# A graph network's attention pass: who tells the DMA queue that a ring slot is free

## The chip, the cores and the metric

The kernel runs on one core of one Trainium2 chip, in one launch. The metric is the device time of that core in microseconds. Three executions of the kernel before took 8953.53, 8963.97 and 8964.85 us; the median is 8963.97 us.

## The reference, cut to what matters

Four graph networks follow each other on 4096 nodes with 256 features and 65536 edges, sorted by target node: five message layers, a weighted graph convolution, an attention layer with 8 heads, and three normalised convolutions, each block closed by `x = layernorm(x + block(x))`. The change touches the attention layer alone:

```
h = (x @ W).reshape(n, 8, 32)
alpha = leaky_relu(a_src[src] + a_dst[dst], 0.2)
ex = exp(alpha - segment_max(alpha, dst)[dst])
coef = ex / (segment_sum(ex, dst)[dst] + 1e-16)
out = segment_sum(h[src] * coef, dst) + bias
```

## The kernel before, in words

The edges are cut into tiles of 128, and 8 tiles make an octet (`U = 8`). There are 64 octets. `ring` holds four octets of gathered rows, one in each slot. Octets are walked by a hardware loop over 16 groups with four octets (`ob`) written out in each.

A sum over edges that share a target is a matrix product with a one-hot matrix: VectorE builds, for a block of 128 target nodes, the matrix "edge e goes to node n", and TensorE multiplies it with the rows. An octet whose targets lie in one block needs one such unit of 8 matmuls, an octet that straddles two blocks needs two. How many blocks an octet touches is data: each engine that needs it loads it from `span_row` into a register (`span_of`, L210 to L219) and branches on it.

The attention layer has two passes over the edges. The first gathers the rows, writes them to `rows_table` and finds each node's maximum. The second, `attend_pass` (L599), reads the rows back octet by octet. Its engines do this:

- SP loads an octet's rows into its slot (L642) as soon as `rows_used` says that the slot is free. TensorE set `rows_used` to 4 at the kernel's start, so the first four loads wait for nothing of this pass.
- VectorE, in step h: multiplies the 8 tiles of octet h by their exponents (L841), adds the sums that TensorE finished last to `AGG` (L786), builds the first one-hot matrices of octet h+2 (`look_up_first`, L629), works out the logits of octet h+1 (`exponents`, L818 to L826), builds the second unit's one-hots of octet h if it has one, adds again, and builds the second unit's one-hots of octet h+2 if it has one.
- ScalarE takes the exponential of octet h+1 (L758) and copies the turned one-hots of octet h+2 out of PSUM (L751).
- TensorE, in step h: six of the eight matmuls of octet h's first unit (`sums`, L712), the transposes of octet h+2's one-hots (`turn_first`, L658), the last two matmuls, a second unit of sums if octet h has one, and then `find_all(h+2)`: it fetches each edge's target values by a product with the turned one-hots. `find_all` loads the octet's span into registers (L679), waits until VectorE has read the bank `psO` for the octet before (`logits`, L683), opens the bank's accumulation with a matmul of zeros (L685), does the products (L670), with another round of transposes where there is a second unit (L690), and closes with a matmul of zeros that signals `octet_found` (L693).

Between the sums of step h and `find_all(h+2)` stands L734, which is the line of the change:

```
pe.drain().then_inc(rows_used, 1)
ahead(pe, i, ob, 2, find_all)
```

The drain holds TensorE's sequencer until all its matmuls are done, and then tells SP that octet h's slot is free. `ahead` leaves `find_all` out in the last two octets. The waits of `attend_pass` on TensorE are on semaphores that VectorE and ScalarE raise (`weighed`, `b_made`, `b_added`, `a_made`, `a_copied`, `logits`).

Of the kernel before, what the change touches and what calls it, by code (L numbers as in the profile page):

```python
# [11 lines left out]
P = 128  # L12
# [10 lines left out]
U = 8  # L23
# [17 lines left out]
def build(nc, x, src, dst, edge_attr, edge_weight, vn_emb0, We, be, W1, b1, W2, b2, bn_g, bn_b, bn_m, bn_v,  # L41
# [3 lines left out]
    with ctx:  # L45
# [3 lines left out]
        def pb(name, shape):  # L49
            return ctx.enter_context(nc.psum_tensor(name, shape, F32))  # L50

        def sem(name):
            return ctx.enter_context(nc.semaphore(name))
# [83 lines left out]
        psO = pb("psO", [P, 512])  # L137
# [22 lines left out]
        rows_used = sem("rows_used")  # L160
# [37 lines left out]
        def flat(ap):  # L198
            return ap.rearrange("p a b -> p (a b)")
# [17 lines left out]
        def span_of(eng, h):  # L217

            v = eng.value_load(span_row[0:1, bass.ds(2 * h, 1)], min_val=NB, max_val=NB * NB + NB - 1)  # L219
            lo = nc.s_assert_within(v & (NB - 1), 0, NB - 1,  # L220
                                    skip_runtime_bounds_check_because="the low bits")
            cnt = nc.s_assert_within(v >> (NB.bit_length() - 1), 1, NB,
                                     skip_runtime_bounds_check_because="1 to NB blocks")
            return eng.snap(lo), eng.snap(cnt)
# [374 lines left out]
        def attend_pass(loads):  # L599
            W = 3 * 2 * HEADS  # L600
            found = small[:, 0:U * 2 * HEADS].rearrange("p (u h) -> p u h", u=U)
            zeros = stk_f[:, 3 * U * P // 2:2 * U * P].bitcast(BF16)[:, 0:U * W]
            turnedS = [psE[:, 512 * g:512 * g + 256].bitcast(BF16) for g in range(2)]

            def high(ap):

                halves = ap.bitcast(BF16).rearrange("p (e two) -> p e two", two=2)
                return halves[:, :, 1:2].rearrange("p e o -> p (e o)")

            def sums_bank(eng, c):  # L610

                start = nc.s_assert_within((c & U) * (512 // U), 0, 512,
                                           skip_runtime_bounds_check_because="0 or 512")
                return psAT[:, bass.ds(eng.snap(start), AW)]

            def in_range(b):
                return nc.s_assert_within(b, 0, NB - 1, skip_runtime_bounds_check_because="a block of the octet")

            def ahead(eng, i, ob, by, work):

                if ob < OB - by:
                    work(i, ob + by)
                else:
                    with eng.If(i < NG - 1):
                        work(nc.s_assert_within(i + 1, 0, NG - 1, skip_runtime_bounds_check_because="i < NG - 1"),
                             ob + by - OB)
# [7 lines left out]
            with nc.Block() as block:  # L634
                @block.sync
                def _(sp):

                    with sp.Fori(0, NG) as i:
                        for ob in range(OB):

                            sp.wait_ge(rows_used, OB * i + ob + 1)
                            sp.dma_start(octet_rows(ob), rows_table[bass.ds((OB * i + ob) * P, P), :]  # L642
                                         ).then_inc(rows_in[ob], 16)
                    loads(sp)

                @block.tensor
                def _(pe):
                    pe.reg_mov(na_pe, 0)
                    pe.reg_mov(nb_pe, 0)
                    pe.reg_mov(nx_pe, 0)  # L650

                    def turn(ob, c):
                        for g in range(2):
                            pe.wait_ge(a_made, c + 4 * g + 4)

                            pe.wait_ge(a_copied, c + 4 * g + 4)
                            for u in range(4 * g, 4 * g + 4):
                                ins = nc.tensor.transpose(turnedS[g][:, P * (u % 4):P * (u % 4) + P],  # L658
                                                          high(S_of[ob][:, u, :]), ident_b[:, :])
                            ins.then_inc(a_turned, 4)  # L660

                    def turn_first(i, ob):

                        turn(ob, pe.snap(na_pe))

                    def find(b, c):
                        for g in range(2):
                            pe.wait_ge(a_copied, c + U + 4 * g + 4)
                            for u in range(4 * g, 4 * g + 4):
                                ins = nc.tensor.matmul(psO[:, W * u:W * (u + 1)], ST[:, P * u:P * u + P],  # L670
                                                       flat(tgt[:, :, :])[:, bass.ds(b * W, W)],
                                                       start=False, stop=False)
                            ins.then_inc(a_found, 4)
                        pe.reg_add(na_pe, na_pe, U)

                    def find_all(i, ob):

                        h = OB * i + ob
                        lo, cnt = span_of(pe, h)  # L679
                        pe.reg_mov(cnt_pe[ob], cnt)  # L680
                        if not (isinstance(h, int) and h == 0):

                            pe.wait_ge(logits, h)  # L683

                        nc.tensor.matmul(psO[:, 0:U * W], zeros[:, 0:P], zeros, start=True, stop=False)  # L685
                        find(lo, pe.snap(na_pe))
                        with pe.If(cnt > 1):
                            with pe.Fori(1, cnt) as j:
                                c = pe.snap(na_pe)
                                turn(ob, c)  # L690
                                find(in_range(lo + j), c)

                        nc.tensor.matmul(psO[:, 0:U * W], zeros[:, 0:P], zeros, start=False, stop=True  # L693
                                         ).then_inc(octet_found, 1)


                    pe.wait_ge(zeros_ready, 1)
                    for ob in range(2):
                        turn_first(0, ob)
                        find_all(0, ob)  # L700
                    with pe.Fori(0, NG) as i:
                        for ob in range(OB):
                            h = OB * i + ob

                            def sums(c, first, u0, u1):
                                bank = sums_bank(pe, c)
                                for u in range(u0, u1):
                                    if first:
                                        pe.wait_ge(weighed, U * h + u + 1)
                                    elif u % 4 == 0:  # L710
                                        pe.wait_ge(b_made, pe.snap(nx_pe) + u + 4)
                                    ins = nc.tensor.matmul(bank, S_of[ob if first else OB][:, u, :],  # L712
                                                           ring[:, U * ob + u, 0:AW],
                                                           start=(u == 0), stop=(u == U - 1))
                                    if u % 4 == 3:
                                        ins.then_inc(b_used, 4)

                            c = pe.snap(nb_pe)

                            pe.wait_ge(b_added, c + U)  # L720
                            sums(c, True, 0, U - 2)

                            ahead(pe, i, ob, 2, turn_first)
                            sums(c, True, U - 2, U)
                            pe.reg_add(nb_pe, nb_pe, U)
                            cnt = pe.snap(cnt_pe[ob])
                            with pe.If(cnt > 1):
                                with pe.Fori(1, cnt):
                                    c = pe.snap(nb_pe)
                                    pe.wait_ge(b_added, c + U)  # L730
                                    sums(c, False, 0, U)
                                    pe.reg_add(nx_pe, nx_pe, U)
                                    pe.reg_add(nb_pe, nb_pe, U)
                            pe.drain().then_inc(rows_used, 1)  # L734
                            ahead(pe, i, ob, 2, find_all)

                @block.scalar
# [1064 lines left out]
```

## Time and profile before

| | us |
|---|---|
| median of three runs | 8963.97 |
| the profiled execution, its own time | 8958.51 |
| its span | 8956.7 |
| TensorE busy with matmuls | 6282.8 (70%) |
| VectorE busy | 4267.3 (48%) |
| GpSimd busy | 5397.4 (60%) |
| the attention pass, from the first slot load to the last sum | 5920 to 6613 |

The span is cut by the passes over the edges, each of which starts after the one before. A wait in one pass counts for that pass alone. Rows begin with the start in us and the duration; PE is TensorE's matmul, PEld its weight load, PEldq its sequencer, DVE VectorE, ACT ScalarE, SPq the queue of SP. "[0.69 <-ACT ...]" is idle time of that engine ahead of the row, and what ended it; "issue" is idle time that no wait seen in the profile explains.

### The profile page before, as it was taken

The numbers are of one execution on the slowest core, as the hardware profiler recorded it, in microseconds if no ns is written. First come the engines' busy times: TensorE is split into PE (matmuls) and PEld (weight loads), VectorE is DVE, ScalarE is ACT, GpSimd is POOL, SyncE is SP. The second block draws the span as 40 slices with busy tenths as digits, with TensorE's granted clock in tenths as the row PEclk, the third lists the DMA queues.
The fourth block names the chain that finished last, engine by engine and source line by source line (L and its number), as shares of the span: only waits on it lengthen the run. The fifth ranks groups of instructions, "written<-read, shape, count | busy, mean of one in ns | idle before, by whom it ended". The sixth has DMA issues, their size and how long they took to land. (4 is left out here: it accounts for less than half of the span.)

```text
span 8956.7 us, 127721 instructions
## 1 busy us (share of the span) xinstructions
PE 6282.8 (70%) x27247; PEld 4638.4 (52%) x27248; DVE 4267.3 (48%) x9200; ACT 1900.8 (21%) x5238; POOL 5397.4 (60%) x5435
## 2 busy tenths in 40 slices
PE   3677877867786787778677445668856776776775
PEld 2456655755574565557345334655643453454443
DVE  6555555455545555555223644567672233234224
ACT  3322333323223233323343100011110000000000
POOL 2776477467737765772777367720027775775776
PEclk9889889989988998899688765579877798898788
DMA  5443244244424433441333046643213332332332
GB/s 167 124 127 109 91 131 127 74 127 129 125 72 132 127 96 107 129 125 61 114 101 100 6 159 213 209 144 110 91 40 103 101 100 87 103 102 83 102 101 87
DMA packets 422112, 993.32 MB, mean 111 GB/s; under 512 B 124049, under 2 KB 188306, under 8 KB 405650
## 3 DMA queue, kind: packets, MB, share of 16 engines
q0 software_dynamic: 246800, 677.71, 25.9%
q1 hardware_dynamic: 175234, 314.77, 10.9%
q8 instruction: 24, 0.39, 0.0%
q14 instruction: 54, 0.44, 0.0%
HBM read 858.79 MB, written 133.30 MB: 111 GB/s over the span
## 5 line engine op out<-in xcount | busy, mean ns | idle before, releaser
L272 POOL DMA_INDIRECT ring<-node_table,idx x4608 | 4536.1, 984 | 1742.8 <-issue 1680.3
L342 PE MATMUL psAT<-ring,S 128*128 128x256 f32 x13680 | 3935.8, 439 | 1108.0 <-DVE AGG L386 510.6
L342 PEld LDWEIGHTS psAT<-ring,S 128*128 128x128 f32 x13680 | 2809.0, 216 | 2204.4 <-issue 918.8
L239 DVE SCALAR_TENSOR_TENSOR S<-iota,block_start,dst_f 128x512 f32<-128x512 f32 x1900 | 1421.4, 748 | 1615.1 <-PE psAT L342 1522.8
L360 ACT ACTIVATE ring<-ring 128x256 f32<-128x256 f32 x2560 | 957.5, 416 | 2216.7 <-DVE ring L401 2211.8
L401 DVE TENSOR_TENSOR ring<-ring,psE 128x256 f32<-128x256 f32 x2560 | 962.7, 416 | 808.6 <-DMA ring<-node_table,idx 712.4
L386 DVE TENSOR_TENSOR AGG<-AGG,psAT 128x256 f32 x864 | 361.3, 418 | 1051.3 <-PE psAT L342 1051.3
L311 PE MATMUL psE<-we_stk,stk 128*128 128x256 bf16 x2560 | 394.0, 282 | 531.9 <-DVE ring L401 436.9
L272 POOL DMA_INDIRECT ring<-att_table,idx x512 | 504.3, 985 | 158.8 <-issue 158.5
L311 PEld LDWEIGHTS psE<-we_stk,stk 128*128 128x128 bf16 x2560 | 204.7, 99 | 751.9 <-DVE ring L401 659.7
L256 ACT COPY idx<-src_i 128x8 int32 x640 | 125.3, 196 | 1997.1 <-DMA ring<-node_table,idx 1976.7
L1714 POOL TENSOR_TENSOR Y<-Y,ex_self 128x2816 f32<-128x2816 f32 x2 | 9.9, 4932 | 741.4 <-ACTq L1541 741.4
L472 PE MATMUL psAT<-picks,S 128*128 128x9 f32 x1520 | 339.9, 363 | 126.4 <-DVE cand L518 126.4
L472 PEld LDWEIGHTS psAT<-picks,S 128*128 128x128 f32 x1520 | 331.3, 330 | 144.7 <-DVE S L239 103.2
L1454 POOL TENSOR_TENSOR tab<-H,be_row 128x256 f32<-128x256 f32 x128 | 105.9, 828 | 445.5 <-DVE H L1451 445.5
L364 ACT ACTIVATE ring<-ring,weight 128x256 f32<-128x256 f32 x512 | 259.5, 508 | 408.6 <-DMA ring<-node_table,idx 408.6
L977 PE MATMUL psE<-tT,w_sb 128*128 128x128 f32 x2560 | 314.0, 276 | 0.9 <-ACT tT L1006 0.8
L990 PE MATMUL psE<-w_sb,hT 128*128 128x256 f32 x1280 | 301.9, 379 | 0.0
L977 PEld LDWEIGHTS psE<-tT,w_sb 128*128 128x128 f32 x2560 | 300.4, 193 | 2.4 <-ACT tT L1006 2.1
L990 PEld LDWEIGHTS psE<-w_sb,hT 128*128 128x128 f32 x1280 | 231.4, 190 | 25.0
L1015 ACT ACTIVATE hT<-psE,b_col 128x128 f32<-128x128 f32 x640 | 182.5, 368 | 227.3 <-PE psE L977 227.3
L964 PE MATMUL psAT<-ident,tin 128*128 128x128 f32 x320 | 66.4, 290 | 222.6 <-DVE tin L203 185.6
(268 smaller groups left out, 4246.1 us busy)
## 6 DMA issues: line engine op xcount, KB each, us to landing
stk<-stack_table SPq DMA_DIRECT2D x320, 256.0 KB, 2.7
ring<-node_table,idx POOLq DMA_INDIRECT x4608, 2.8
rows_table<-ring SPq DMA_DIRECT2D x64, 1072.0 KB, 4.7
ring<-rows_table SPq DMA_DIRECT2D x64, 1072.0 KB, 4.9
node_table<-tab SPq DMA_DIRECT2D x224, 128.0 KB, 1.7
stack_table<-stk SPq DMA_DIRECT2D x64, 256.0 KB, 2.0
ring<-att_table,idx POOLq DMA_INDIRECT x512, 3.0
w_sb<-in_L_gnn_W SPq DMA_DIRECT2D x10, 512.0 KB, 10.6
```

What stands on the lines that cost most here:

```text
L239: nc.vector.scalar_tensor_tensor(S[:, 4 * g:4 * g + 4, :], iota[:, :].unsqueeze(1).to_broadcast([P, 4, P]), block_start[:, bass.ds(blk, 1) ...
L272: nc.gpsimd.indirect_dma_start(ring[:, q, 0:gw], None, table, bass.IndirectOffsetOnAxis(ap=idx[:, q:q + 1], axis=0)).then_inc(gathered[q], 16)
L311: ins = nc.tensor.matmul(psE[:, D * u:D * u + D], stk[:, ob, P * u:P * u + P], we_stk[:, :], start=True, stop=True)
L342: ins = nc.tensor.matmul(psA[:, 0:D], S[:, u, :], ring[:, q, 0:D], start=(u == 0), stop=(u == U - 1))
L360: nc.scalar.activation(ring[:, q, 0:D], ring[:, q, 0:D], ACT.Relu).then_inc(message, 1)
L364: nc.scalar.activation(ring[:, q, 0:D], ring[:, q, 0:D], ACT.Copy, scale=weight[:, bass.ds(RING * i + q, 1)]).then_inc(message, 1)
L386: return nc.vector.tensor_tensor(a, a, psA[:, 0:D], ALU.add)
L401: nc.vector.tensor_tensor(ring[:, q, 0:D], ring[:, q, 0:D], psE[:, D * u:D * u + D], ALU.add).then_inc(pre_added, 1)
L472: ins = nc.tensor.matmul(psA[:, (HEADS + 1) * u:(HEADS + 1) * (u + 1)], S[:, u, :], picks[:, U * half + u, :], start=True, stop=True)
L977: ins = nc.tensor.matmul(psE[:, 512 * q + P * j:512 * q + P * j + P], w1_sb[:, f, P * j:P * j + P], tT[:, q, P * f:P * f + P], start=(f == ...
L990: ins = nc.tensor.matmul(result_of(q), a, w, start=(n == 0), stop=(n == len(terms) - 1))
L1015: ins = nc.scalar.activation(hT[:, q, P * j:P * j + P], psE[:, 512 * q + P * j:512 * q + P * j + P], ACT.Relu, bias=b1_col[:, j:j + 1])
```

## The change

The drain goes. The increment of `rows_used` is hung on the opening matmul of zeros of the next `find_all`, which TensorE finishes after all the sums that were issued ahead of it. The two calls of `find_all` ahead of the loop, which follow no sums, don't raise it. In the last two octets, where `find_all` isn't called, nothing raises it any more; SP's last load waits for 64, and 4 + 62 are raised.

```
-                    def find_all(i, ob):
+                    def find_all(i, ob, frees=True):
                         h = OB * i + ob
                         lo, cnt = span_of(pe, h)
...
                             pe.wait_ge(logits, h)
-                        nc.tensor.matmul(psO[:, 0:U * W], zeros[:, 0:P], zeros, start=True, stop=False)
+                        ins = nc.tensor.matmul(psO[:, 0:U * W], zeros[:, 0:P], zeros, start=True, stop=False)
+                        if frees:
+                            ins.then_inc(rows_used, 1)
...
                     for ob in range(2):
                         turn_first(0, ob)
-                        find_all(0, ob)
+                        find_all(0, ob, False)
...
-                            pe.drain().then_inc(rows_used, 1)
                             ahead(pe, i, ob, 2, find_all)
```

## Rows read from the trace of the kernel before

**Rows 1.** Busy time by engine in most of the attention pass (PE, PEld, DVE, ACT, POOL, clock)

```profile
5950.00:6600.00 650.00, 529.49 (x3050) 389.26 (x3051) 444.64 (x1070) 114.66 (x246) 0.00 (x0) 0.90 0.29 103
```

**Rows 2.** Waits, 5940 to 6600: who, for whom, total us, times, longest

```profile
PE psO L685 <- issue: 73.2, 62, 1.3
DVE AGG L786 <- PE psAT L712: 73.2, 40, 4.5
DVE w_sb L629 <- PE psE L658: 32.9, 18, 4.7
...
PE psO L670 <- ACT stk L751: 21.4, 32, 0.7
...
DVE small L818 <- PE psO L693: 9.1, 19, 1.2
PE psE L658 <- issue: 9.1, 31, 0.3
DVE S L629 <- PE psE L658: 8.0, 7, 3.7
...
DVE stk L629 <- PE psE L658: 7.4, 6, 3.8
...
DVE hT L629 <- PE psAT L712: 0.9, 3, 0.3
```

**Rows 3.** TensorE's sequencer: the drain, the span's load; ns min/median/max, first and last start

```profile
L734 PEldq DRAIN  x64: 2133/3624/3970, 5944.5 to 6608.4; - x64
```

```profile
L219 PEldq TENSOR_LOAD <-span_row x64: 297/309/320, 5932.1 to 6591.1; - x64
```

**Rows 4.** Timeline of PE, the first opening, which no drain precedes

```profile
5931.42 1.27 PE L658 MATMUL psE<-ident_b,S 128*128 128x128 bf16 x8 [21.78 <-DVE S L629]
5932.91 0.49 PE L685 MATMUL psO<-stk 128*128 128x384 bf16 x1 [0.23 <-issue]
```

**Rows 5.** Timeline, an octet with one unit that finds one

```profile
5981.48 1.11 PE L712 MATMUL psAT<-ring,stk 128*128 128x265 f32 x4
...
5983.72 0.33 PE L685 MATMUL psO<-stk 128*128 128x384 bf16 x1 [1.13 <-issue]
5983.73 0.42 DVE L786 TENSOR_TENSOR AGG<-AGG,psAT  x1
...
5984.49 1.41 DVE L629 SCALAR_TENSOR_TENSOR S<-iota,block_start,dst_f 128x512 f32<-128x512 f32 x2 [0.34 <-issue]
...
5985.02 2.94 PE L712 MATMUL psAT<-ring,w_sb 128*128 128x265 f32 x12
5985.83 0.55 DVE L818 TENSOR_REDUCE small<-psO 128x128 f32<-128x384 f32 x1
...
5987.06 0.23 DVE L826 TENSOR_TENSOR al<-al,small 128x64 f32<-128x64 f32 x1
...
5987.87 2.77 DVE L841 TENSOR_TENSOR ring<-ring 128x256 f32<-128x256 f32 x8 [0.59 <-ACT ring L758]
...
5990.56 0.42 DVE L786 TENSOR_TENSOR AGG<-AGG,psAT  x1
```

**Rows 6.** Timeline, an octet with two units that finds two

```profile
6243.75 0.33 PE L685 MATMUL psO<-stk 128*128 128x384 bf16 x1 [1.09 <-issue]
...
6246.08 0.72 PE L670 MATMUL psO<-tgt,stk 128*128 x8 [0.69 <-ACT stk L751]
...
6247.13 4.30 PE L712 MATMUL psAT<-ring,w_sb 128*128 128x265 f32 x12
...
6253.26 0.43 DVE L786 TENSOR_TENSOR AGG<-AGG,psAT  x1 [2.75 <-PE psAT L712]
```

**Rows 7.** Timeline of PE, the first and the last slow six matmuls, and a typical one

```profile
6014.77 4.43 PE L712 MATMUL psAT<-ring,w_sb 128*128 128x265 f32 x12
...
6215.68 4.63 PE L712 MATMUL psAT<-ring,w_sb 128*128 128x265 f32 x12
...
6585.03 4.32 PE L712 MATMUL psAT<-ring,stk 128*128 128x265 f32 x12
```

**Rows 8.** Timeline, the copies after a one-unit octet's transposes, and the last of its sums

```profile
6220.59 1.11 PE L712 MATMUL psAT<-ring,w_sb 128*128 128x265 f32 x4
6220.69 1.07 ACT L751 COPY stk<-psE 128x512 bf16<-128x512 bf16 x2 [3.33 <-PE psE L658]
```

**Rows 9.** Line 642, the slot's load, from issue to landing

```profile
DMA to landing us min/median/max: 4.8/4.9/10.9
```

## The prediction

> **What bounds the kernel now.** The change lives in the attention pass, so I read that stretch first by busy time: from 5950 to 6600 us TensorE is busy 529 of 650 us, VectorE 445, ScalarE 115, GpSimd not at all [rows 1]. TensorE leads, but 82% is no proof. The table of waits says more: TensorE's idle time there is 73.2 us before the opening matmul of `find_all` (62 times, about 1.18 us each), 21.4 us for ScalarE's copies, 9.1 us before transposes, and none worth naming for VectorE. VectorE on the other hand waits for TensorE 73.2 + 32.9 + 9.1 + 8.0 + 7.4 + 0.9 = 131.5 us [rows 2]. So TensorE sets the pace of the pass and the gap before the opening is its largest idle term. The second reading is the clock: the pass has a mean of 0.90, not 1 [rows 1]. Six matmuls of sums (12 records) take 2.94 us in a good octet [rows 5] and 4.3 to 4.6 in a slow one [rows 7]. The matmul's step doubles from one of the two levels, 2.4 GHz, to the other, 1.2 GHz, for a part of those six.
>
> **What the drain costs.** TensorE's sequencer stands at the drain for 2133 to 3970 ns, median 3624 [rows 3]: it is that far ahead of the array. When the array is empty it starts from nothing with the span's load (309 ns [rows 3]), the register work, the wait on `logits` and the opening. In the timeline the sums' last records end at 5981.48 + 1.11 = 5982.59 and the opening starts at 5983.72, so the gap is 1.13 [rows 5]. Without the drain the sequencer does all that while the array works off what was issued. That it can is shown by the kernel's own first opening, which has no drain ahead of it: the transposes run from 5931.42 to 5932.69, the load starts at 5932.1, beside them, and the gap is 0.23 although the transposes were issued only as they ran [rows 3, 4]. With a lead of over 2.1 us against a start of about 1.2 us, the gap should go to nothing. The wait on `logits` stays where it was and isn't late: the logits for the opening at 5990.6 ended at 5987.29 [rows 5]. Removed from TensorE: 62 gaps, 73 us.
>
> The Trainium skill, "Advanced Engine Details and Errata", Sequencer Loop and Engine Queue Depths, says that engine instructions are pushed into a queue while control instructions run beside them, and gives TensorE's queue 64 places. By that rule the whole gap goes; the trace agrees as far as it shows a lead of 3.6 us [rows 3].
>
> **What the increment costs.** It rides on a matmul that exists. The slot is told free at the end of the opening instead of at the end of the sums, so it is 0.33 us after the array gets there instead of about 0.1. The load takes 4.9 us [rows 9], and its rows are wanted three octets later, over 20 us. Cost nothing; if that cover were gone, at most the 1.2 to 1.5 us per octet by which the release could move, priced under the rivals.
>
> **What is late next.** A gap of TensorE is worth only what VectorE can follow. Between two openings I compared three numbers of the two timelines, for the 61 windows in the loop: the gap at the end, the slow clock's share, and VectorE's idle time that TensorE ended. By class (units found, units summed) the means are:
> - one, one: 16 windows of 7.24 us, gap 1.16, VectorE waits 0.82, 3 with slow clock. The smaller of gap and wait, taken window by window, sums to 7.8 us. In the steady run VectorE has no wait on TensorE left: 0.42 for the add, 1.41 for the one-hots, 1.46 from L818 to the end of L826, 0.58 through ScalarE and 2.77 for the products make 6.64 of a round of 6.83 (5983.73 to 5990.56) [rows 5].
> - one found, two summed: 15 windows of 10.52 us, gap 1.21, wait 1.03, none slow; 14.4 us.
> - two found, one summed: 16 windows of 10.73 us, gap 1.18, wait 3.13, all slow; 18.5 us.
> - two, two: 14 windows of 14.1 us, gap 1.19, wait 3.63 (in the one shown 2.75 of it at L786 [rows 6]), 13 slow; 16.7 us.
>
> Sum of the first term: 7.8 + 14.4 + 18.5 + 16.7 = 57.4 us.
>
> **The clock.** In 32 windows the six matmuls are slow, each by about 4.63 − 2.94 = 1.69 us [rows 5, 7]. Nearly all follow a find of two units: the gap (1.1 to 1.3), 0.28 before the transposes, 0.69 for ScalarE [rows 2, 6], and short matmuls between. Windows that find one unit have the gap alone, and the clock stays at 2.4 GHz. Without the gap the find of two leaves 0.97 us idle, less than the 1.13 that a find of one carries at full clock [rows 5]. If every slow stretch went, VectorE's waits would let through 4.0 + 0 + 18.8 + 23.0 = 45.8 us more, by the same comparison. The bounds of this term are 0 and 45.8. I take the two/two class (23.0) and the three one/one windows (4.0): 27. For the class with one unit summed I take none, because a new wait comes in there, next.
>
> The Trainium skill, "TensorE: Matmul & The Clock Gate", section on the second HAM failure mode, says that frequent short idles between groups of matmuls make the clock swing. By it the sum would move toward the upper bound as idles go; the trace agrees in that only the finds of two, which have the most such idles, are slow [rows 6, 7].
>
> **The new wait.** In a one-unit octet the copies of the turned one-hots end at 6221.76, and the sums at 6221.70 [rows 8]. Today the 1.2 us gap covers them. Without it the opening runs at once, 0.33 us, and the products behind it need the copies plus a wake-up of about 0.2 us (the second half of rows like the 0.69 one [rows 6]). The sequencer also does the branch and the closing matmul only after that wait, with no lead. Bounds: 0 and about 0.8 us in each of 32 octets, 0 to 26 us; where VectorE bounds the octet it costs nothing. I take 0.3, 10 us, nearer to the row's near-tie.
>
> **The sum.** 57 + 27 − 10 = 74 us off. The profiled execution's own time is 8958.5 (span 8956.7), so it would become 8884. It lies 5.5 below the median of the runs, 8964, for which I forecast 8889.
>
> **The rivals.**
> - The gap goes and the clock stays as it is, since the waits that come in (ScalarE's copies, VectorE's second one-hots) are idle time too: 57 − 10 = 47 off, 8917. For it: 32 regular slow stretches whose idle only partly goes.
> - All slow stretches go and the new wait is hidden: 57 + 46 = 103 off, 8861. For it: VectorE's 131.5 us of waits leave room [rows 2]. Against it: the near-tie [rows 8].
> - The change doesn't do what it says: the span's load or the registers hold the sequencer anyway, and the gap shrinks by the drain's own turn-round alone, some 0.15 us of it: 62 x 0.15 = 9 us, 8955. Against it: the opening without a drain [rows 4].
> - Slower: TensorE, no longer the bound, waits in more places, each short, and stretches that run at 2.4 GHz now fall to 1.2. The place is the 31 windows that find one unit; one slow stretch costs 1.69. It decides when the loss passes the 47 of the first rival, that is if all 31 turned slow and the one-unit octets lost as much again in their second sums: 2 x 31 x 1.69 = 105, less 47, is 58 slower, 9022. Against it: these windows hold the clock with 1.1 to 1.3 us idle today. A late slot (62 x 1.5 = 93) would need over 20 us of lead to vanish.
>
> **How the numbers follow.** Forecast, 65 to 90 us off: 0.45. Clock unchanged, 39 to 65 off: 0.23. All of it, over 90 off: 0.14. Only a remainder, 18 to 39 off: 0.05. Not doing what it says: 0.08. Slower: 0.05. What a measurement of this kernel tells from no change is 0.2%, 18 us. So faster 0.45 + 0.23 + 0.14 + 0.05 = 0.87, same 0.08, slower 0.05. The range runs from 8855, 103 off with the runs' own spread of some 6 us, to 8928, the clock rival with its new wait a little dearer (36 off).
>
> **What would show it.** In the profile after, L734's drain is gone and the idle before L685 falls from 73 us to under 10. VectorE's waits for TensorE fall from 131 to 50 to 70. The idle before L670 that ScalarE ends rises above 21. The slow six-matmul stretches fall from 32 to about half, and the pass's clock rises from 0.90 to about 0.95. One-unit octets settle near 6.7 us. Slot loads still land long ahead of use. I am wrong if the gap before the opening stays, if the time leaves the attention pass, or if VectorE's waits stay where they are while TensorE's idle only moves.

## The result, and the profile after

The changed kernel takes 8847.91 us in the median of four runs (8847.43 to 8859.57) against 8960.06 us before (four runs as well): 112 us less, a ratio of 0.9879 with a 95% interval of 0.9867 to 0.9892. The direction was forecast, the size was not: 8889 was the forecast, and the time lies below the range's 8855.

The gain is in the attention pass. I measure the pass from the first opening matmul to the end of VectorE's last add, two rows of the timeline. Before, it ran from 5932.91 to 6613.19, 680.3 us. After the change its two ends are these rows of the timeline:

```profile
5939.98 0.49 PE L685 MATMUL psO<-stk 128*128 128x384 bf16 x1 [0.23 <-issue]
```

```profile
6504.34 0.43 DVE L788 TENSOR_TENSOR AGG<-AGG,psAT  x1 [3.14 <-PE psAT L715]
```

That is 564.8 us, 115.5 less. The profiled execution (8859.57 us, the slowest of the four by 11.5 us) spent 16.6 us more than the one before outside this pass. In eight other profiles on chips of this speed, one of them with the drain in place, that part is 1 to 10 us longer than in the profile of the kernel before, so I take it for scatter. The pass carries the whole gain, and I compare passes from here on.

How far can one pass be trusted? A second profile of the same changed kernel gave 561.8 us. Kernel 15 below has the same attention pass line for line, on another chip, and there it took 573.1 us (7398.18 to 7971.30), with 12 slow stretches where the first profile has 8 and the second 6. So a difference under about 10 us between passes of two chips says nothing by itself; beside passes of the same chip it says more.

The busy row of the pass answers to [rows 1]; its sixth column is the clock:

```profile
5950.00:6500.00 550.00, 481.48 (x3114) 370.55 (x3113) 448.55 (x1095) 116.02 (x249) 0.00 (x0) 0.97 0.35 122
```

VectorE's busy time is what it was, 448.6 against 444.6 us, in a shorter stretch. The granted clock rose from 0.90 to 0.97. The waits of 5947 to 6490 answer to [rows 2]:

```profile
PE psO L670 <- ACT stk L753: 33.5, 47, 1.0
...
DVE AGG L788 <- PE psAT L715: 15.8, 20, 1.6
PE psAT L715 <- DVE hT L629: 14.4, 17, 1.3
...
DVE w_sb L629 <- PE psE L658: 7.3, 5, 1.7
...
DVE hT L629 <- PE psAT L715: 2.6, 8, 0.4
...
PE psO L685 <- DVE al L828: 2.0, 5, 0.5
...
DVE S L629 <- PE psE L658: 1.3, 1, 1.3
...
DVE stk L629 <- PE psE L658: 1.3, 1, 1.3
```

The 73.2 us of "issue" before L685 are gone. VectorE's waits for TensorE fell from 131.5 to 28 us, where 50 to 70 had been forecast, and TensorE now waits for VectorE's second one-hots (14.4 us), which it did not before. TensorE was the bound alone; now the two share that.

A two-unit octet that finds two shows both halves of the gain. The timeline of TensorE, to be laid beside [rows 6]:

```profile
6367.30 0.33 PE L685 MATMUL psO<-stk 128*128 128x384 bf16 x1
6367.46 0.36 PE L670 MATMUL psO<-tgt,stk 128*128 x8
6367.66 0.61 PE L658 MATMUL psE<-ident_b,w_sb 128*128 128x128 bf16 x8
6368.96 0.66 PE L670 MATMUL psO<-tgt,stk 128*128 x8 [0.69 <-ACT stk L753]
...
6370.00 2.94 PE L715 MATMUL psAT<-ring,w_sb 128*128 128x265 f32 x12
```

The opening follows the sums with no gap, the 0.28 us before the transposes that the kernel before has there went too, and although the 0.69 us for ScalarE stay, the six matmuls of sums take 2.94 us where they took 4.30. By class of window between two openings (units found, units summed), from both engines' timelines; a slow stretch is one in which the first six matmuls of sums take well over 2.94 us:

| class | windows | us before | us after | slow stretches before, after |
|---|---|---|---|---|
| one, one | 16 | 7.24 | 6.06 | 3, 1 |
| one, two | 15 | 10.52 | 9.84 | 0, 0 |
| two, one | 16 | 10.73 | 8.33 | 16, 6 |
| two, two | 14 | 14.10 | 10.98 | 13, 1 |

Times the number of windows, the classes gained 19, 10, 38 and 44 us, 111 together; the rest of the 115.5 lies ahead of the first of these windows and behind the last. On TensorE, the idle time in this stretch fell from 116 to 63 us, and the time covered by its instructions from 527 to 468 us, of which the sums are 45.

### The profile page after: what moved, and what is told of

Its sections match the earlier page's. It is cut to its first block and busy times, and to the rows that moved or that the text cites. A ratio compares the mean times of both kernels' runs of the same rounds, so it can differ in the third digit from the quotient of the medians.

```text
span 8857.8 us, 127657 instructions
## 1 busy us (share of the span) xinstructions
PE 6236.9 (70%) x27247; PEld 4625.8 (52%) x27248; DVE 4268.9 (48%) x9200; ACT 1905.0 (22%) x5238; POOL 5415.5 (61%) x5435
```

## The experiments

Kernel 1 is the kernel of experiment 1, and so on; kernels 1 to 4 ran on one chip, 5, 7, 8 and 9 on a second, 6, 10, 12 and 13 on a third, 11, 14 and 15 on a fourth. A ratio is the time over that of the kernel before on the same chip; the pass is from the profile. The first and the fourth chip took 22 and 24% longer outside the attention pass (10.8 and 10.9 ms in all, both the kernel before and its variants); there the totals scatter by 0.5%, the same 112 us are a ratio of 0.990, and mainly the pass is read. They are called scattering below, the others steady. The profile of the kernel before, 680.3 us, is from a chip of 8.96 ms.

**1. A drain that raises nothing, ahead of the changed find_all.**

```
+                            pe.drain()
                             ahead(pe, i, ob, 2, find_all)
```

> The slot is freed by the opening matmul as in the changed kernel, but a drain that raises nothing stays ahead of find_all. If the gain comes from the sequencer running ahead (my theory), all of it goes: within 10 us of the kernel before, about 8960, gap before the opening again about 1.15 us, 32 slow stretches. If where the slot is freed matters, most of the 112 us stay.

Pass 675.1 us, ratio 0.9999 (0.9970 to 1.0028). The waits of TensorE:

```profile
PE psO L685 <- issue: 71.0, 62, 1.3
```

With the drain back in, the gap, the slow stretches (33) and the time are those of the kernel before. Where the slot is freed gives nothing.

**2. The span's load ahead of the drain, in the kernel before.** `load_span` holds the load and the register work that `find_all` had at its start; `find_all` takes the values from registers.

```
+                            ahead(pe, i, ob, 2, load_span)
                             pe.drain().then_inc(rows_used, 1)
                             ahead(pe, i, ob, 2, find_all)
```

> The kernel before with its drain, but the span of the next octet is loaded into registers ahead of the drain. If the gap is the control work behind the drain (load 0.31 us and register work), it falls from 1.18 us to about 0.4, 62 x 0.75 = 46 us of TensorE's idle time go; with the idle time shorter some slow stretches may go too: 8905 to 8930. If the gap is the drain's own turn-round, nothing is gained: about 8955 to 8960.

Pass 604.5 us, ratio 0.9938 (0.9909 to 0.9967), on a scattering chip. The waits of TensorE and the drain's row:

```profile
PE psO L692 <- issue: 20.5, 62, 0.5
```

```profile
L743 PEldq DRAIN  x64: 13/1824/3682, 7363.6 to 7951.1; - x64
```

The gap is down to 0.33 us each, and two thirds of the gain (76 of 115 us; 71 against kernel 1 on the same chip) are there with the drain still in. The drain's own turn-round is the small part. What costs is the load and the register work that have to stand behind it. With 53 us less idle time the clock fell less often too: 19 slow stretches are left of 32. The 40 us that the changed kernel is faster still are these 20.5 us of gap and 11 slow stretches more, in the main.

**3. and 4. Four matmuls of zeros while TensorE waits for the copies, in the kernel before and in the changed one.** They add zeros to `psO`, so the result stays.

```
                                 turn(ob, c)
+                                for _ in range(4):
+                                    nc.tensor.matmul(psO[:, 0:U * W], zeros[:, 0:P], zeros, start=False, stop=False)
                                 find(in_range(lo + j), c)
```

> The kernel before, with four more matmuls of zeros into psO in each second-unit find, in the 0.69 us in which TensorE waits for ScalarE's copies. The drain and its gap stay. If the clock falls because of the idle time in finds of two units, the 32 slow stretches go and the pass gains the clock's share alone, 35 to 50 us: 8910 to 8925. If the fall is the drain's gap or follows something else, the stretches stay slow and the time stays at 8960, or rises by a few us for the added work.

> The changed kernel with the same four matmuls of zeros. 8 slow stretches are left in the changed kernel; if their cause is the idle time for ScalarE, they go, and up to 8 x 1.5 = 12 us are gained where VectorE can follow: 8838 to 8848. If VectorE bounds the pass by now, the same time, 8848; if the added matmuls delay the products, up to 10 us slower.

Before with the fill: pass 637.4 us, ratio 0.9971 (0.9943 to 1.0000). Changed with the fill: 557.6 us, ratio 0.9908 (0.9879 to 0.9937). In the first the gap is untouched and the clock is not; here are its waits and its busy row:

```profile
PE psO L685 <- issue: 73.4, 62, 1.3
```

```profile
7330.00:7930.00 600.00, 498.43 (x3129) 364.76 (x3128) 437.80 (x1055) 113.34 (x243) 0.00 (x0) 0.98 0.31 111
```

More work, 43 us less time by the pass (38 against kernel 1 on the same chip); the totals, 10750 against 10793 us, agree but hardly rise above their scatter. All 29 slow stretches behind a find of two units are gone. That idle time in the find of two brings the clock down there is shown. It is not the only way: 7 slow stretches as long as the others (4.57 to 4.63 us) came up in windows that find one and sum two, where the kernel before has none, and why is open. At nearly equal clock (0.98 in both) the gap is then worth 637.4 − 557.6 = 79.8 us. The gap's rows are 73.4 against 1.9 us. Two things can make up the difference: the openings of the changed kernels start 0.16 us ahead of the recorded end of the sums in the median (matmuls overlap, and their ends are modelled), and slow stretches still cost 14 us in kernel 3 and 7 in kernel 4. They were not separated.

**5. Slots loaded two octets later.**

```
-                            sp.wait_ge(rows_used, OB * i + ob + 1)
+                            sp.wait_ge(rows_used, OB * i + ob + 3)
```

> The changed kernel, but SP waits for two more increments of rows_used before it loads a slot, so that each load starts two octets later. If a load of 4.9 us has over 20 us of room, the pass (first opening to last sum) stays at 565 us within 3 us. If where the slot is freed matters, an octet waits for its rows and the pass grows by tens of us.

Pass 685.5 us, ratio 1.0005 (0.9995 to 1.0015): the first branch of the expectation failed, and the whole gain was lost. The waits between 5960 and 6490 us name it; over the whole pass this one is 87.0 us, 47 times:

```profile
DVE small L820 <- DMA ring<-rows_table: 66.5, 36, 2.5
```

From an opening to the logits that need the rows whose load it sets off there are 16.0 us at the least and 21.6 in the median of the changed kernel (15.6 and 24.4 before), not "over 20". Counted in the changed kernel, two octets later leave 3.3 us of that at the least and 3.4 in the median, for a load of 4.9 us. The wait is less than the 121 us lost: the pass's clock is down to 0.87 too, and TensorE waits 50 us for VectorE's second one-hots.

**6. Slots loaded one octet later** (`+ 2`).

> The changed kernel with each slot load one octet later. From an opening to the logits that need the slot's next rows there are at least 16.0 us in the changed kernel (median 21.6); one octet later at least 9.6. The load takes 4.9 us. If room is all that counts, the pass stays at 565 us within 5 us. Two octets later, where about 3 us were left, it was 686; if the load's place matters otherwise, tens of us are lost here too.

Pass 561.7 us, against 561.8 for the changed kernel on this chip; ratio 0.9872 (0.9852 to 0.9891). One octet later still leaves 9.6 us at the least for a load of 4.9, and there the moment of release is free.

**7. The transposes after four matmuls of sums instead of six, changed kernel.**

```
-                            sums(c, True, 0, U - 2)
+                            sums(c, True, 0, U - 4)
                             ahead(pe, i, ob, 2, turn_first)
-                            sums(c, True, U - 2, U)
+                            sums(c, True, U - 4, U)
```

> The changed kernel with the transposes of octet h+2 after four matmuls of sums instead of six, so that ScalarE's copies are done 0.93 us earlier. If the new wait on the copies (32.7 us before L670, 21 in the kernel before) costs time, its growth of 12 us goes, and the pass falls from 565 to 553 to 560 us. If VectorE bounds the windows in which it stands, the wait shrinks and the pass stays at 565 within 3 us; if the transposes now wait for VectorE's one-hots, it grows by up to 10 us.

Pass 554.9 us, ratio 0.9872 (0.9852 to 0.9891, two runs). That is 7 to 10 us under the changed kernel's two profiles, which are from other chips; the total doesn't show it, and kernel 13 is better evidence. Whatever came did not come from the wait it was made for: L670 still waits 30.3 us for the copies (32.7 before the move, first to last loop opening). VectorE's waits fell from 28 to 17 us, what the slow stretches cost from 15 (10 in the second profile) to about 7.

**8. and 9. VectorE's span load ahead of its wait for the exponents, in the kernel before and in the changed one.**

```
+                            ahead(dve, i, ob, 2, load_span_dve)
                             dve.wait_ge(exps, h + 1)
```

> The kernel before, with VectorE's own load of the span moved ahead of its wait for the exponents. Drain and gap stay. If VectorE was held by that load behind its wait for the sums (one-hots start 1.9 us after the sums' end in each one-unit window), VectorE's idle time put down to issue, 41 us before L629, falls under 15, and TensorE, which bounds the pass, lets the pass gain little: 665 to 678 us against 680. If VectorE's load held the one-unit windows as much as TensorE's gap did, 20 us or more are gained, under 660.

> The changed kernel with the same move of VectorE's load. If VectorE bounds the changed kernel's pass in the windows with one unit found, its 41 us of issue before L629 fall and the pass falls from 565 to 540 to 555 us, about 8825 to 8838 on the scale of 8848. If TensorE bounds it, the pass stays within 3 us of 565.

Pass 681.8 us and 572.0 us; ratios 1.0009 (0.9998 to 1.0019) and 0.9889 (0.9873 to 0.9906). The idle time before the one-hots that no wait explains fell from 41 to 17 and from 41 to 13 us, but nothing was gained: neither expectation's gain came, and the second pass is 7 to 10 us longer than the changed kernel's two, within what two chips can differ by. Its waits:

```profile
DVE ring L848 <- issue: 52.6, 42, 2.1
```

The load outlasts ScalarE's exponential, so the idle time moved from the one-hots to the products (2.1 us there in the changed kernel). The place was wrong, and the question stayed open.

**10. and 11. The same load behind the eight products, ahead of the wait for the sums.**

```
                                     ALU.mult).then_inc(weighed, 1)
+                            ahead(dve, i, ob, 2, load_span_dve)
                             add_sums()
```

> The changed kernel with VectorE's load of the span behind its eight products and ahead of its wait for the sums. Ahead of the wait for the exponents the load cost more than it gave (572 us against 565; idle before the products 53 us). If VectorE's control work bounds the windows that find one unit, the 40 us of issue before L629 go without that price and the pass falls to 540 to 555 us. If TensorE's own chain bounds them, it stays within 5 us of 565.

> The kernel before, drain and gap in place, with VectorE's load of the span behind its eight products. If VectorE's load was a bound of its own in the kernel before, the pass falls from 680 to 660 us or below. If TensorE alone set the pace there, the pass stays within 5 us of 680, and VectorE's 41 us of issue only turn into waits for TensorE. Read with the changed kernel (563) and with the changed kernel that has the move (546): the drain is worth 117 us without the move, and by the second theory 134 with it.

Changed kernel with the move: pass 546.1 us, 8824.85 us in the median, ratio 0.9850 (0.9833 to 0.9866); on this chip that is 15.7 us less pass and 15.4 us less time than kernel 12. Kernel before with the move: pass 678.8 us, ratio 1.0001 (0.9977 to 1.0025). The waits of VectorE in the latter:

```profile
DVE AGG L786 <- PE psAT L712: 83.9, 41, 4.6
```

With the drain in, the load's time only turned into more waiting for TensorE (145 us in all where it had been 129, loop openings only). With the drain gone, it bounds.

**12. The changed kernel itself once more**, on the chip of 6, 10 and 13.

> The changed kernel once more, beside the next three on one chip: about 0.988 of the kernel before, pass 565 us within 5 us. It tells how far a pass read from one profile can be trusted.

8840.21 us, ratio 0.9863 (0.9846 to 0.9879), pass 561.8 us. (Kernel 15's pass widens what this one says of the scatter, see the result.)

**13. Early transposes and the matmuls of zeros together, and 14. these two and VectorE's load behind the products.**

> The changed kernel with both earlier transposes (pass 555) and the four matmuls of zeros (558). If each takes another part, the clock's rest and VectorE's wait for the turned one-hots, the gains of 10 and 7 us add: 545 to 550 us and about 8832 on the scale of 8848. If both gain by keeping the clock up, one is enough: 553 to 557.

> The changed kernel with VectorE's load behind its products (546 us by itself), the transposes two matmuls earlier and the matmuls of zeros (551 together). If they take different parts, the 17 and 12 us add: pass 530 to 538, about 8812 on the scale of 8840 for the changed kernel. If one of VectorE's busy 448 us and TensorE's work bounds the rest, 540 to 546.

Pass 551.2 us, 8832.83 us, ratio 0.9855 (0.9839 to 0.9872), 10.6 and 7.4 us under kernel 12 on the same chip; and 535.2 us, ratio 0.9869 (0.9820 to 0.9918) on a scattering chip. The busy row of the last:

```profile
7430.00:7920.00 490.00, 456.47 (x3053) 346.08 (x3052) 422.22 (x1033) 109.64 (x235) 0.00 (x0) 1.00 0.38 134
```

The clock is full, TensorE is busy for 93% of the pass and VectorE for 86%. By the pass this is the best version, 27 us under the changed kernel's second profile and 38 under kernel 15's pass on the same chip. By total time the lowest ratio measured is that of run 10, 0.9850, whose interval still touches the changed kernel's own; no total of the last version was taken on a steady chip.

**15. The count loaded ahead of the drain in the ten edge passes, changed kernel.**

```
                             units(pe, None, cnt, unit)
+                            load_count((h + 1) & (NO - 1))
                             pe.drain().then_inc(octet_free, 1)
```

> The changed kernel, with the same idea carried to the ten edge passes, whose drain stays: TensorE loads the next octet's number of blocks ahead of the drain instead of behind it. There GpSimd's eight gathers of 1.26 us set the pace of an octet with one block; TensorE's idle time falls by up to 0.3 us in each of 576 octets. If the pace is GpSimd's, nothing: within 0.2% of the changed kernel. If TensorE's gap is part of the chain in octets with two blocks, up to 0.3 x 280 = 84 us are gained.

10805.04 us, ratio 0.9889 (0.9837 to 0.9941), 106 us less than the kernel before, where the changed kernel had 112 and 119 less on other chips. 84 us more would be 0.8% and can be ruled out; under about 0.5% nothing can be said. It ran on a scattering chip, so this stays open for a steady one.

## Why the prediction was wrong

The mechanism was right and the three terms of the sum were mis-sized, all the same way: 57 + 27 − 10 = 74 was forecast, 115.5 was measured in the pass. By class of window (units found, units summed) the sum, with the new wait spread over the one-unit finds, gives 7, 10, 19 and 40 us; 19, 10, 38 and 44 were measured. So the miss sits in two places: windows that find one and sum one (12 us), where the cap and the new wait took too much off, and windows that find two and sum one (20 us), where the clock's term had been put at nothing.

**The gap goes.** Right. The lead of the sequencer covers load, registers and opening; of 62 gaps 2 us are left. Kernel 1 shows that nothing else of the change matters, kernel 2 that it is mostly the control work behind the drain and not the drain's turn-round, as the working had it. By the rule on queues that the prediction took from the Trainium skill ("Advanced Engine Details and Errata", Sequencer Loop and Engine Queue Depths) the whole gap goes; the trace agrees with 2.0 us left of 73.2, and those are waits for VectorE.

**The cap by VectorE, the first term of the sum (57).** This is the first step that failed. It took, window by window, the smaller of gap and VectorE's visible wait. At equal clock the gap is worth about 80 (kernels 3 and 4), 73 if the 7 us that slow stretches cost more in kernel 3 are taken off. Two things were left out. A window with little wait need not lose what the next one with 3.6 us can use; that is argued, no run tests it alone. And "VectorE has no wait on TensorE left" in the one-unit run was a misreading of [rows 5]: the 0.34 us of "issue" ahead of the one-hots are not work. The sums ended at 5982.59, the one-hots began at 5984.49, 1.90 later. The next sums end at 5988.24 + 1.11 = 5989.35, and the next one-hots start at 5991.26, 1.91 later. VectorE's sequencer (DVEq) stood at its wait for the sums and loaded the span only then; here is its load between 5984 and 5992, 0.65 us behind the sums' end:

```profile
L219 DVEq TENSOR_LOAD <-span_row x1: 308/308/308, 5990.0 to 5990.0; - x1
```

Moved ahead, with the drain kept, that time reappears as a wait for TensorE and the pass doesn't change (kernel 11), so before the change it was TensorE's, and removable. In the changed kernel VectorE's add starts at 5989.20 and its one-hots at 5989.55:

```profile
5989.20 0.43 DVE L788 TENSOR_TENSOR AGG<-AGG,psAT  x1
5989.55 1.41 DVE L629 SCALAR_TENSOR_TENSOR S<-iota,block_start,dst_f 128x512 f32<-128x512 f32 x2
...
5995.60 0.43 DVE L788 TENSOR_TENSOR AGG<-AGG,psAT  x1
```

The round is 6.40 us where 6.64 had been given as VectorE's floor and 6.83 was measured before: nearly all of the 0.43 us less is between the add and the one-hots (0.35 instead of 0.76), and the 6.64 counted rows that overlap one after the other. In other windows VectorE's load still stands behind its wait (over the pass this idle time before the one-hots is 41 us before the change and after it), and there it bounds after the change: moving it gives 16 us more (kernel 10 against 12), and with it the drain is worth 133 us instead of 115 (kernels 10 and 11).

**The clock (27).** This is the other step that failed. What is left of 115.5 after the gap's 80 is 36. Counted another way, the slow stretches cost 58 us over 2.94 each before and 15 after, 43 less. The bounds had been 0 and 45.8. The forecast gave the class that finds two and sums one nothing (18.8 had been its bound), on the argument that a new wait would keep it idle; 10 of its 16 slow stretches went (12 in the second profile), and it gained 38 us where 18.5 had been forecast. The new wait came in and did not keep the clock down. In all, 32 slow stretches became 8, where about 16 had been forecast. Idle time in the find does bear on the clock, as kernel 3 shows, and removing the gap ahead of it was mostly enough. The Trainium skill's section on the second HAM failure mode ("TensorE: Matmul & The Clock Gate"), which the prediction drew on, would move the sum to the upper bound as short idles go; the trace agrees with the direction, at 36 to 43.

**The new wait (−10).** As a wait it came at its size: L670 waits 33.5 us for ScalarE, 12 more than before. What it costs was not measured by itself. The other two terms, at 80 and 36, leave nothing to subtract, and the cap had already limited these windows to what VectorE could follow, so the −10 was counted twice; that is argued. Kernel 7 was to test it and could not: with the transposes moved forward the wait hardly fell.

**The slot's room.** "Over 20 us" was wrong at the low end, 16.0, without effect here; kernels 5 and 6 show where it would have had one.

**The rivals.** Not doing what it says and slower are excluded by the result. "All slow stretches go", 103 off, was nearest, at a chance of 0.14, though 8 of the 32 stayed: its number is near because the gap was worth more than its 57.

## What to carry to other kernels

Here a drain cost little by itself (a gap of 0.33 us, kernel 2); count what the sequencer must do behind it before the engine's next instruction (here 1.2 us with the load), and look at how long it stands at the drain: a long stay is a lead that is being thrown away. Try loads of registers ahead of the wait or drain that closes a step, but not ahead of one on which the critical work hangs: kernel 10 gained 16 us by it, kernel 9 nothing. Idle time marked "issue" right behind a wait on another engine can belong to that engine when the room is counted, as kernel 11 showed here.

## What was not expected of the hardware

Adding work made the kernel before faster: 124 matmuls of zeros in idle time took about 40 us off its pass, with the gap as it was, and brought the granted clock from 0.90 to 0.98. Without them, two idles of 0.28 and 0.69 us and a gap of 1.1 to 1.3 us, with short matmuls between, stood ahead of the fall to 1.2 GHz in 29 of 30 finds of two units. Two chips took 22 and 24% longer outside the attention pass (10.8 and 10.9 ms in all), with the same length of that pass within 5 us (675.1 and 678.8 against 680.3). There the mean granted clock of the whole program was 0.78 to 0.80 where it was 0.84 to 0.85 on the others, and GpSimd waited 1453 us for the edge passes' drains in 334 places (kernel 1), where it waited 56 us in 9 places before. Which is cause and which is effect was not studied.
